# Two expert stages of a gated cross-attention network: mixture weights through DRAM instead of a matmul, and a three-deep order of work

## The reference

```python
shared = jax.nn.silu(x @ sg_w.T) * (x @ su_w.T) @ sd_w.T
scores = jax.nn.sigmoid(x @ gate_w.T) + gate_bias
...                                     # keep the best 4 of 8 groups, then the best 6 experts
topk_w = topk_w / (topk_w.sum(axis=-1, keepdims=True) + 1e-08)
comb = jnp.zeros((T, E), x.dtype).at[jnp.arange(T)[:, None], topk_i].add(topk_w)
h = jax.nn.silu(jnp.einsum('th,eih->eti', x, eg_w)) * jnp.einsum('th,eih->eti', x, eu_w)
routed = jnp.einsum('eti,ehi,te->th', h, ed_w, comb)
return (shared + routed).reshape(B, S, H)
```

## Time and profile before

| | |
|---|---|
| median of 3 runs | 680.71 us (679.11 to 683.18) |
| the profiled execution | 680.45 us, of which the span of the profile is 678.3 us |
| busy in the span | PE 613.6, DVE 397.2, ACT 385.9, POOL 195.1 us |
| mean TensorE clock granted | 0.957 of full speed |
| stage 1, first to last matmul of L647 to L649 | about 101.1 to 155.4 us |
| stage 7, the same | about 505.1 to 675.0 us |
| mean DMA rate over the span | 27 GB/s |

### The profile page before, as it was taken

The page is one execution under the profiler, slowest core; times in us unless marked ns, Lnnn a source line. Parts: engine busy times, 40 slices in busy tenths (PEclk is TensorE's granted clock), DMA queues, the critical chain, the costliest instruction groups (busy, mean ns, idle before and its releaser), DMA issues.

```text
span 678.3 us, 10957 instructions
## 1 busy us (share of the span) xinstructions
PE 613.6 (90%) x3608; PEld 411.4 (61%) x3608; DVE 397.2 (59%) x750; ACT 385.9 (57%) x759; POOL 195.1 (29%) x189
## 2 busy tenths in 40 slices
PE   9999986899699997888797998899986899999997
PEld 6467764676554444666453444467654678878885
DVE  2278838567642446666226565378859465565665
ACT  4477864555445335888653444477872555656653
POOL 4000022770000000000000344000022677787775
PEclk9999979899679999999979999899987899999999
DMA  8100001110000000000000001000000122211110
GB/s 286 65 1 2 2 15 33 31 48 1 0 1 0 0 1 0 1 3 1 1 0 0 25 23 61 1 3 1 2 32 16 31 63 62 62 47 49 59 31 32
DMA packets 9611, 18.57 MB, mean 27 GB/s; under 512 B 1856, under 2 KB 3024, under 8 KB 9440
## 3 DMA queue, kind: packets, MB, share of 16 engines
q1 hardware_dynamic: 9568, 18.01, 8.5%
HBM read 17.48 MB, written 0.52 MB: 27 GB/s over the span
## 4 chain that ended last, share of the span: by engine, by line
PE 81%; DVE 8%; issue 5%; ACT 4%; POOL 1%; ACTq 0%; DVEq 0%; POOLq 0%
PE bank L647 8%; PE bank L648 8%; PE bank L649 8%; PE bank L564 4%; PE bank L575 4%; PE bank L894 3%; PE bank L590 3%; PE bank L526 3%; PE bank L489 3%; PE bank L664 3%; PE bank L908 2%; PE bank L538 2%; PE bank L883 2%; PE bank L1004 2%; PE bank L860 2%
## 5 line engine op out<-in xcount | busy, mean ns | idle before, releaser
L402 POOL TENSOR_TENSOR h_lo<-wc,h_hi 128x512 fp32r<-128x512 f32 x82 | 105.9, 1293 | 75.1 <-ACT h_hi L1232 74.7
L1224 ACT ACTIVATE wa<-bank 128x512 f32<-128x512 f32 x84 | 50.3, 599 | 85.5 <-PE bank L649 85.5
L1636 DVE TENSOR_TENSOR wb<-wa,bank 128x512 f32<-128x512 f32 x80 | 54.8, 688 | 67.5 <-PE bank L649 52.4
L647 PE MATMUL bank<-xn_hi,w_hi 128*128 128x512 f32 x168 | 69.0, 411 | 10.8 <-DVE wc L1628 6.1
L648 PE MATMUL bank<-xn_lo,w_hi 128*128 128x512 f32 x168 | 66.9, 398 | 0.0
L649 PE MATMUL bank<-xn_hi,w_lo 128*128 128x512 f32 x168 | 66.7, 397 | 0.0
L1643 DVE TENSOR_TENSOR wc<-wb,bank 128x512 f32<-128x512 f32 x80 | 54.8, 687 | 10.2 <-PE bank L664 5.8
L1232 ACT ACTIVATE h_hi<-wc 128x512 fp32r<-128x512 f32 x84 | 52.3, 624 | 13.0 <-DVE wc L1628 4.9
L1445 DVE TENSOR_REDUCE row_max<-bank 128x4 f32<-128x512 f32 x64 | 43.6, 682 | 20.3 <-PE bank L564 19.6
L430 POOL TENSOR_TENSOR x<-x,upd 128x128 f32 x16 | 7.3, 455 | 150.7 <-ACT upd L1101 150.7
L1449 DVE TENSOR_TENSOR wa<-bank,row_max 128x512 f32<-128x512 f32 x64 | 44.3, 692 | 7.6 <-ACT wb L1114 4.4
(11 more groups left out here) (270 smaller groups left out, 1273.1 us busy)
## 6 DMA issues: line engine op xcount, KB each, us to landing
ring<-in_experts SPq DMA_DIRECT2D x42, 256.0 KB, 2.6
ring<-in_experts SPq DMA_DIRECT2D x8, 192.0 KB, 2.5
mats<-in_mats SPq DMA_DIRECT2D x1, 1472.0 KB, 10.1
mats<-in_mats SPq DMA_DIRECT2D x1, 832.0 KB, 6.2
mats<-in_mats SPq DMA_DIRECT2D x2, 320.0 KB, 8.2
x<-in_x_t SPq DMA_DIRECT2D x1, 512.0 KB, 4.0
...
```

The costliest lines, as they stand in the source:

```text
L402: nc.gpsimd.tensor_tensor(h_lo[:, k % 2, :], wc[:, k % 2, :], h_hi[:, k % 2, :].bitcast(f32), ALU.subtract).then_inc(m_h_lo, 1)
L647: mm(out, w, x_, start=start, stop=False)
L1224: fn(wa[:, k % 2, :], bank[k % 2][:, :], ACT.Silu).then_inc(m_silu, 1)
L1636: v.tensor_tensor(wb[:, par, :], wa[:, par, :], bank[2 + par][:, :], ALU.mult).then_inc(m_t, 1)
```

## The change

The matmul `weight` goes. The mixture weights no longer get split in two parts; DVE's last routing operation writes them straight to `comb_pieces`, PE transposes them into banks 6 and 7, ACT copies only the rows that hold experts to `comb_t`, now plain fp32. SP then stores `comb_t` in DRAM (`comb_rows`, one row of 4 KB per expert), waits for it, and reads for each pair two rows back, each to 64 partitions at once, into one of four slots of `pair_w` (two DMAs of 256 KB a pair). The block of selecting columns is no longer loaded or split, so a pair's weights are 192 KB instead of 256 KB.

PSUM is dealt out anew: three banks for gate, three for up, two for the result. `silu` writes back to the gate bank it reads. DVE multiplies the up bank by `pair_w` first (`weighed`), then by the bank that holds the silu (`gated`). `h_hi`, `h_lo` and the hidden values have three buffers each. `down` runs three units behind `gate_up`, the pairs go one after the other, and the hardware loop is gone: all units are written out. ACT now does `hidden` of a unit before `silu` of the next one.

```diff
@@ memory
-            nc.alloc_sbuf_tensor_at(name, [P, 2, HALF], f32r, offset=arena_at + 16384 + k * 4096)
-            for k, name in enumerate(("xn_hi", "xn_lo", "h_hi", "h_lo")))
+        h_hi, h_lo = (nc.alloc_sbuf_tensor_at(name, [P, 3, HALF], f32r, offset=arena_at + 4 * 12288 + k * 6144)
+                      for k, name in enumerate(("h_hi", "h_lo")))
-        comb_t = sb("comb_t", [P, T], f32r)
+        comb_t = sb("comb_t", [P, T])
+        pair_w = arena[:, 8192:12288].rearrange("p (s t) -> p s t", s=4)
+        comb_rows = [nc.dram_tensor(f"comb_rows{n}", (e, T), f32).ap() for n, e in enumerate((16, 64))]
...
+        def slot_of(q):
+            return (q + 3) % 4
+        def hidden_of(v):
+            return wa[:, 0, :] if v % 3 == 2 else wc[:, v % 3, :]
@@ SP: moe_rest
-                with sp.Fori(1, m["rounds"]) as i:
...
+                def pair_weights(q):
+                    slot = slot_of(q)
+                    for j in range(2):
+                        row = comb_rows[n][2 * (q - 1) + j:2 * (q - 1) + j + 1, :]
+                        sp.dma_start(pair_w[64 * j:64 * j + 64, slot, :], row.to_broadcast([64, T]))\
+                            .then_inc(pair_in[slot], 16)
+                for q in range(4, 7):
+                    refill(q)
+                sp.wait_ge(m_combE, 4 * n + 2)
+                sp.dma_start(comb_rows[n], comb_t[0:m["E"], :]).then_inc(m_rows, 16)
+                sp.wait_ge(m_rows, 16 * (n + 1))
+                for q in range(1, 5):
+                    pair_weights(q)
+                for q in range(5, pairs + 1):
+                    if q + 2 <= pairs:
+                        refill(q + 2)
+                    sp.wait_ge(m_t, products_done(m, 2 * (q - 4) + 1))
+                    pair_weights(q)
@@ POOL: moe
-                hidden_rest(0, u0, n > 0)
-                rest(1, q0 + 2)
-                hidden_rest(1, u0 + 1, n > 0)
...
+                rest(2)
+                hidden_rest(0)
+                hidden_rest(1)
+                rest(3)
+                for v in range(2, m["units"] - 1):
+                    hidden_rest(v)
+                    if v % 2 == 0 and v >= 4 and v // 2 + 2 <= m["pairs"]:
+                        rest(v // 2 + 2)
@@ PE: moe
-                def weight(slot, c, k, unit):
-                    if not isinstance(unit, int) or unit >= u0 + 4:
-                        pe.wait_ge(m_h, unit - 1)
-                    mm(bank[4 + k % 2][:, :], w_hi[:, slot, 384:512], comb_t[:, c * HALF:c * HALF + HALF],
-                       start=True, stop=True).then_inc(m_cb, 1)
...
+                for v in range(5):
+                    gate_up(v)
+                for c in range(2):
+                    combine_t(c)
+                for v in range(2):
+                    pe.wait_ge(m_combE, 4 * n + v + 1)
+                    down(v)
+                for v in range(5, m["units"]):
+                    gate_up(v)
+                    down(v - 3)
+                for v in range(m["units"] - 3, m["units"]):
+                    down(v)
@@ PE: gate_up, in the new form
+                    pe.wait_ge(m_w_lo, q0 + q + 1)
+                    if v < 2:
+                        pe.wait_ge(m_x_lo[c], n + 1)
+                    if v >= 3:
+                        pe.wait_ge(m_h, u0 + v - 2)
@@ ACT: moe
+                def silu(v):
+                    act.wait_ge(m_g, u0 + v + 1)
+                    fn(bank[v % 3][:, :] if v >= 2 else wa[:, v, :], bank[v % 3][:, :], ACT.Silu).then_inc(m_silu, 1)
...
+                for v in range(2, m["units"]):
+                    hidden(v)
+                    if 5 <= v + 1 < m["units"]:
+                        silu(v + 1)
+                    if v % 2 == 0 and v >= 4 and v // 2 + 2 <= m["pairs"]:
+                        split(v // 2 + 2)
@@ DVE: route_weights and moe
-                split_weights(picked, E).then_inc(m_comb, 2)
...
+                    v.tensor_tensor(pieces, picked, share, ALU.mult).then_inc(m_comb, 2)
...
+                def weighed(unit):
+                    dve.wait_ge(m_u, u0 + unit + 1)
+                    dve.wait_ge(pair_in[slot], pair_fills(m, q))
+                    dve.wait_ge(m_h, u0 + unit - 1)
+                    v.tensor_tensor(wb[:, c, :], pair_w[:, slot, c * HALF:c * HALF + HALF],
+                                    bank[3 + unit % 3][:, :], ALU.mult).then_inc(m_t, 1)
+                def gated(unit):
+                    dve.wait_ge(m_silu, u0 + unit + 1)
+                    dve.wait_ge(m_t, products_done(m, unit))
+                    if unit >= 3:
+                        dve.wait_ge(m_h_lo, u0 + unit - 2)
+                    v.tensor_tensor(hidden_of(unit), wb[:, unit % 2, :], bank[unit % 3][:, :], ALU.mult)\
+                        .then_inc(m_h, 1)
...
-                gated(0, u0 + 2)
-                gated(1, u0 + 3)
                 route_weights(m)
+                for unit in range(2, m["units"]):
+                    weighed(unit)
+                    gated(unit)
```

245 lines of the change are left out of this document (84 added, 161 removed).

## The result

The changed kernel takes 675.49 us (median of 6 runs, 670.55 to 676.85) beside 680.12 for the kernel before (679.11 to 683.18): ratio 0.993 (0.990 to 0.996). A second series of the same kernel gave 673.81 beside 681.14, ratio 0.990 (0.986 to 0.993), so the gain is 4.6 to 7.3 us. The forecast was 667.8. The sign and the range held; the gain forecast, 12.9 us, was about twice what came (1.8 to 2.8 times, by the series).

A forecast was written before the change was run, and what follows sets the result against it. PE's matmuls were taken as the bound. Stage 7 (-13.0 - 2.0 + 1.8 = -13.2) and stage 1 (-2.0 + 2.4 = +0.4) gave -12.8 us from 680.45: 667.6, predicted as median 667.8, range 662 to 676.

The forecast's parts named there:

- The steady part: Restart to T (last `gate_up` ends): each unit loses one of ten matmuls, -13.0 us in stage 7, -2.0 in stage 1.
- slips: Small PE delays in stage 7 where the loop turns and `w_lo` comes late; taken as gone, -2.0 us, at worst 0.
- Rival A: The ACT and DVE ring through `silu`, now writing PSUM, becomes the bound: 672 us if `silu` takes 0.80; chance 10%.
- The tail: From the end of the last `gate_up` through the last products to `down`: unchanged at 4.1 us.
- the lock: DVE's routing operation on two SBUF operands slows beside POOL's moved third `rest`: 0.8 us a stage, between 0 and 1.0.
- the restart: Where PE's matmuls go on after each routing: forecast 1.8 us later in stage 7, 2.4 us later in stage 1.
- copy behind the routing: From DVE's last routing operation to the end of ACT's copy: 1.84 us in stage 7, 1.9 in stage 1.
- store, loads, waking up: Weights' trip through DRAM in each stage: store 2.0, pair 1's two loads 3.3, waking up 0.1, together 5.4 us.
- `weighed` and `gated`: DVE's two products of unit 2, between the landing of pair 1's weights and unit 5's `gate_up`: 1.4 us.
- matmuls after the restart: PE starts again at the lower clock after idling, as before: 1.6 us in each stage, so no change.
- Rival B: The DRAM round trip is longer, loads 5.2 and store 3, costing 3 us in each stage: 673.8 us; chance 12%.
- everything between the two stages: The stretch from stage 1's end to stage 7's start should take as long as before, to within 0.5 us.

The follow-up runs named there:

- e4: The kernel before with its stage 7 hardware loop written out, nothing else changed: 680.19 us, ratio 1.000.
- e12: The changed kernel run again unaltered, as base of the experiments: 673.81 us over 12 runs, ratio 0.990.
- e10: The changed kernel, but in stage 7 one 512 KB DMA per pair reads one row to all 128 partitions: 674.00 us, ratio 0.988.
- e1: The changed kernel, but loads of pairs 2 to 4 are held back until pair 1 has landed: 673.93 us, ratio 0.991.
- e6: The changed kernel, but each stage 7 load of `pair_w` reads 64 distinct rows instead of one row 64 times: 673.96 us, ratio 0.989.
- e11: The changed kernel, but ACT issues the second row of pairs 1 to 4 on its own queue: 671.83 us, ratio 0.988.
- e3: The changed kernel, but pair 1's weights are spread by PE matmuls and copied by ACT, without DRAM: 665.12 us, ratio 0.978.
- e2: The changed kernel with unused filler matmuls keeping PE busy ahead of the transposes and behind them: 669.39 us, ratio 0.986.

## Why the prediction was wrong

The steps that held:
- **The steady part.** A unit is 2.04 us, PE never waits between restart and T, POOL and DVE stay hidden, SP's loads of `pair_w` are never waited for. Matmuls were to give -13.0 us and slips -2.0 in stage 7; restart to T fell from 140.72 (from the first `down`, 530.24 in the earlier trace rows) to 126.40, -14.3. e4 shows 1.3 us of the slips to be the loop's.
- **Rival A** had no ground: `silu` in PSUM is 18 ns shorter, not 200 longer. The Trainium skill, ScalarE: Activation LUTs, "Step-by-step: what each stage is for", which the prediction cited, has PSUM as the faster destination; this trace agrees, by 581 ns against 599.
- **The tail**, 4.07 us both times, and **the lock**, 0.69 us in stage 7 (1.38 against 0.69) where I took 0.8.

The step that failed is the restart. It was to come 1.8 us later in stage 7 and 2.4 in stage 1 (measured from the stage's start, to the point where PE goes on); it came 5.9 and 4.4 later. With the loss behind it, term by term, measured less forecast:

| term | forecast | stage 7 | stage 1 |
|---|---|---|---|
| copy behind the routing | 1.84, 1.9 | +0.8 | +0.7 |
| store, loads, waking up | 5.4 | 7.98, +2.6 | 6.90, +1.5 |
| `weighed` and `gated` | 1.4 | +0.2 | +0.2 |
| routing's end, other terms | | +0.6 | -0.4 |
| matmuls after the restart | 1.6 for the clock | +0.7 | +1.0 |

Together 7.9 us by the rounded terms; the difference between -12.8 and -5.05 is 7.75. e12 divides it otherwise in small things: 4.2 us for the trip through DRAM, 2.0 for the copy and the matmuls (those of stage 1 lose nothing there), and stage 1's routing is 0.7 later than forecast and not 0.4 earlier. So the first step below is firm at 4.1 to 4.2 us, the second lies between 2.0 and 3.2.

1. **The trip through DRAM was mis-sized: 4.1 us.** The store took 2.9 instead of 2.0 in stage 7, and two loads of half the partitions, up to `weighed`, 5.05 instead of 3.3 and 0.1. My rows all come from transfers of all 128 partitions. For such a load the forecast was right: e10's, of 512 KB, lands in 3.4 us. The two of pair 1 take 4.6, so 1.2 us are the halves; the sentence that two loads to disjoint halves are worth what one of 512 KB is did not hold here. e1 shows that 0.2 to 0.4 are the queue behind; e6 excludes the repeated row and e11 the single queue. From the landing to `weighed` the trace of stage 7 has 0.45 us where I took 0.1 (stage 1: 0.08); why is open. The store reads 64 partitions, and the 2.0 of the earlier trace rows is a store of the same size from 128; that this makes its 0.9 us agrees with e10, and no run tests it. In stage 1 the store took 1.9, as forecast, though the 1.8 us that I quoted for it is a load in the earlier trace rows; all of its 1.5 us are the loads. e3 shows the mechanism by taking the trip away.

   Rival B (5.2 and 3, 3 us a stage) gave 673.8 and had 12%. That the median lies there is luck: B had the trip cost 6 us more than the forecast, where it cost 4.1 more, and nothing more for the clock. Its store of 3 us was right for stage 7. Its reason for the loads, that the second waits for the first, was not: the second lands 1.1 us behind the first.
2. **The change of the clock was put at nothing: 3.2 us (2.0 in e12).** The prediction says that the clock falls in the gap as it did, 1.6 us each again. It falls earlier: the shared pair's `down` and unit 5's `gate_up` now stand behind the transposes, so PE idles 6.06 us ahead of them instead of 1.25, the transposes run at 1.2 GHz, 0.88 us longer on the chain, and after 7.75 us more of idleness 12 matmuls run at the lower clock, 5.26 us instead of 2.73. By e2 all of it is worth 5.8 us in the two stages (4.7 beside e12), where the forecast had twice 1.6; the 3.2 are the copy and matmul rows of the table. e2 fills the idle time with other matmuls; no run puts the moved work back, so that this work was what kept the clock up is argued from the two timelines.

The rest is the routing's end and the two products, 0.6 us. The prediction also said that everything between the two stages would take as long as before, to within 0.5 us; it took 3.5 us less, and from 345.1 to 351.1 over the eleven traces, so that sign could not tell anything.
